# A decoder layer on one core: the order in which an instruction's waits are written

## What is computed

```
x = x + attn(layernorm(x))         # 16 heads, q and k are products of two linear maps, causal within a chunk
x = x + mixer(ctx, layernorm(x))   # conv, softplus step sizes, scan over 512 steps with 16 states, gate silu(z)
x = x + ffn(layernorm(x))          # bit_linear(silu(gate) * val), weights rounded to -1, 0, 1

def step(state, inp):              # the mixer's scan
    d, b, c, u = inp
    dA = jnp.exp(d[..., None] * A)
    state = state * dA + (d * u)[..., None] * b[:, None, :]
    y = jnp.einsum('bdn,bn->bd', state, c)
    return (state, y)
```

## Time and profile before

| | |
|---|---|
| median of 3 runs | 981.41 us (980.48 to 981.87) |
| span of the profiled execution | 979.3 us |
| TensorE busy | 811.0 us, 83% |
| VectorE busy | 790.5 us, 81% |
| ScalarE busy | 591.0 us, 60% |
| GpSimd busy | 478.2 us, 49% |
| chain that ended last | TensorE 47%, VectorE 28%, ScalarE 17% |

### The profile page before, as it was taken

One profiled execution on the slowest core, in us unless ns is written; L12 is line 12 of the kernel. 1 busy time (PEld: TensorE's weight loads), 2 busy tenths in 40 slices (PEclk: granted clock), 3 DMA queues, 4 the chain that ended last, 5 costly groups with the idle time before them and its releaser, 6 DMA issues.

```text
span 979.3 us, 11629 instructions
## 1 busy us (share of the span) xinstructions
PE 811.0 (83%) x4036; PEld 451.5 (46%) x4036; DVE 790.5 (81%) x932; ACT 591.0 (60%) x865; POOL 478.2 (49%) x283
## 2 busy tenths in 40 slices
PE   5778887548398888997988798998789899998798
PEld 2335555333263434565464344655455345664354
DVE  5879777577798988878798888787789998876874
ACT  3779779973457766355366766353356785533443
POOL 0447865685427534474347543356445645562020
PEclk8789797758699999988999899999799999999799
DMA  8676786867345543676535463565733555673000
GB/s 297 239 218 188 200 260 197 236 176 196 76 84 122 126 87 86 152 151 159 110 66 129 98 129 65 142 133 123 163 76 76 122 120 129 147 151 76 1 12 33
DMA packets 50495, 130.93 MB, mean 134 GB/s; under 512 B 7203, under 2 KB 7587, under 8 KB 50437
## 3 DMA queue, kind: packets, MB, share of 16 engines
q0 software_dynamic: 16128, 58.73, 31.6%
q1 hardware_dynamic: 34308, 71.45, 22.7%
HBM read 67.09 MB, written 4.35 MB: 73 GB/s over the span
## 4 chain that ended last, share of the span: by engine, by line
PE 47%; DVE 28%; ACT 17%; issue 6%; DMA 2%; DVEq 0%; SPq 0%; ACTq 0%
PE bank L839 18%; DVE W L1828 8%; PE bank L1054 6%; DVE PB L1817 5%; PE bank L868 4%; PE bank L887 4%; PE bank L1071 3%; ACT DEC L1294 3%; DVE U L1786 3%; DVE BST L1763 2%; PE bank L924 2%; PE bank L907 2%; PE bank L946 2%; DVE ARENA L1858 2%; DVE HAM L1974 1%
## 5 line engine op out<-in xcount | busy, mean ns | idle before, releaser
L1670 POOL TENSOR_TENSOR W<-W,CROW 128x1024 f32<-128x1024 f32 x128 | 317.6, 2481 | 226.4 <-DVE W L1828 195.9
L1828 DVE TENSOR_TENSOR_SCAN W<-DEC,PB 128x1024 f32<-128x1024 f32 x125 | 285.8, 2286 | 5.3 <-DVE PB L1817 1.0
L1817 DVE TENSOR_TENSOR PB<-DU,PB 128x1024 f32<-128x1024 f32 x128 | 156.5, 1223 | 21.6 <-PE PB L1009 17.5
L1683 POOL DMA_DIRECT2D ACC<-W x112 | 98.4, 878 | 146.7 <-DMA ACC<-W 124.9
L1294 ACT ACTIVATE DEC<-DT,ACOL 128x511 f32<-128x511 f32 x250 | 160.1, 710 | 15.1 <-DVE W L1828 14.1
L1054 PE MATMUL bank<-W,ARENA 128*128 128x512 fp8e4 x512 | 127.6, 394 | 0.0
L1249 ACT ACTIVATE ARENA<-bank 128x512 f32<-128x512 f32 x56 | 33.0, 593 | 90.3 <-PE bank L887 46.0
L1054 PEld LDWEIGHTS bank<-W,ARENA 128*128 128x128 bf16 x512 | 46.2, 100 | 64.4 <-issue 21.9
L1392 ACT ACTIVATE ARENA<-bank,SDQ 128x512 f32<-128x512 f32 x64 | 43.4, 686 | 47.5 <-PE bank L1054 47.2
L1966 DVE SCALAR_TENSOR_TENSOR ARENA<-bank,SDQ,ARENA 128x512 f32<-128x512 f32 x64 | 47.1, 741 | 27.1 <-ACT ARENA L1392 10.0
L868 PE MATMUL bank<-IDF,ARENA 128*128 128x128 f32 x384 | 55.2, 288 | 15.2 <-DVE ARENA L1845 5.9
(11 more groups left out here) (170 smaller groups left out, 1326.0 us busy)
## 6 DMA issues: line engine op xcount, KB each, us to landing
ACC<-W POOLq DMA_DIRECT2D x112, 512.0 KB, 4.6
CROW<-c_rows SPq DMA_DIRECT2D x98, 256.0 KB, 3.6
W<-in_wffn SPq DMA_DIRECT2D x27, 512.0 KB, 6.8
X<-in_wffn SPq DMA_DIRECT2D x21, 512.0 KB, 5.4
X<-in_x SPq DMA_DIRECT2D x7, 1024.0 KB, 8.8
out_dram<-X SPq DMA_DIRECT2D x16, 256.0 KB, 2.1
X<-in_ctxT SPq DMA_DIRECT2D x4, 512.0 KB, 5.1
ARENA<-in_x SPq DMA_DIRECT2D x1, 1024.0 KB, 5.8
```

Source lines behind the costliest of these rows:

```text
L1670: pool.tensor_tensor(w, w, CROW[k % 2][:, :].unsqueeze(1).broadcast_to([P, 2, L]), ALU.mult)\
L1683: pool.dma_start(ACC[accumulator(u)][:, :, :], w, accum_op=ALU.add).then_inc(y_summed, 16)
L1817: dve.tensor_tensor(into, du, rows, ALU.mult).then_inc(dbu_done.sem, 1)
L1828: dve.tensor_tensor_scan(flat(W[u % 4]), flat(decay_of(u)), flat(PB[:, scan_bank(u):scan_bank(u) + 2, :]), 0.0, ALU.mult, ALU.add).then_in ...
```

## The change

No instruction of an engine is added, removed or moved. Only waits are: the order in which they are written ahead of an instruction is turned around in some fifteen places, some are left out where an earlier one covers them, and on GpSimd some are written ahead of another instruction. The diff, cut to what the prediction speaks of (`reversed(...)` is put around the lists of drained banks in `up` and `largest` too, and `project_first`, `tile_T`, `scales_T`, `attend` and `gate_mixer` swap two waits in the same manner):

```
 def product(key, terms, ready=()):
-    for r in (R.free_at(*key), *ready):
+    for r in (*ready, R.free_at(*key)):
         pe.wait_ge(*r)
...
 def transposes(key, source, ready):
-    for r in (R.free_at(*key), *ready):
+    for r in (*ready, R.free_at(*key)):
...
 def kv(b, g):
-    for r in (R.free_at(*key), R.drained_at(b, "kfT", g), R.drained_at(b, "v", g)):
+    for r in (R.drained_at(b, "kfT", g), R.free_at(*key), R.drained_at(b, "v", g)):
...
 def abs_sums(i):
+    if i:
+        act.wait_ge(abs_done, i)
     act.wait_ge(w_abs[i % len(ABS_STAGE)], 16 * (i // len(ABS_STAGE) + 1))
-    act.wait_ge(abs_done, i)
...
 def outputs_c(u):
...
     b, h, n = unit(u)
+    if u < PAIRED and n % 2 == 0:
+        return
+    if transfers(u) > 1:
+        pool.wait_ge(y_summed, 16 * (transfers(u) - 1))
     pool.wait_ge(*hc_done.at(0, u + 1))
-    if opens(u):
+    if u == half_units(b, h)[1 if u < PAIRED else 0]:
         pool.wait_ge(*y_init.at(b, 2 * h + 2))
     if u < PAIRED:
-        if n % 2 == 0:
-            return
         pool.tensor_tensor(w, w, W[(u - 1) % 4][:, :, :], ALU.add).then_inc(pair_added, 1)
         pool.wait_ge(pair_added, u // 2 + 1)
-    if transfers(u) > 1:
-        pool.wait_ge(y_summed, 16 * (transfers(u) - 1))
     pool.dma_start(ACC[accumulator(u)][:, :, :], w, accum_op=ALU.add).then_inc(y_summed, 16)
...
 def inputs_b(u):
-    dve.wait_ge(*b_bcast.at(0, SPREAD_OF[u] + 1))
-    dve.wait_ge(*du_ready.at(b, 2 * h + 2))
+    if u:
+        dve.wait_ge(*scan_done.at(0, u))
+    if not joined(u):
+        dve.wait_ge(*b_bcast.at(0, SPREAD_OF[u] + 1))
+    if opens(u):
+        dve.wait_ge(*du_ready.at(b, 2 * h + 2))
...
-    if u:
-        dve.wait_ge(*scan_done.at(0, u))
...
 def feature(b, g, i):
+    dve.wait_ge(*R.drained_at(b, one, g))
     dve.wait_ge(*R.full_at(b, two, g))
-    dve.wait_ge(*R.drained_at(b, one, g))
...
 def gated(f, t, c):
+    if t and c == 2:
+        dve.wait_ge(*R.full_at(f, "hT", t - 1, 1))
+        dve.wait_ge(*R.full_at(f, "hT", t - 1, 0))
+    dve.wait_ge(*R.drained_at(f, "G", t, c))
     dve.wait_ge(*R.full_at(f, "V", t, c))
-    dve.wait_ge(*R.drained_at(f, "G", t, c))
-    if t and c == 2:
-        dve.wait_ge(*R.full_at(f, "hT", t - 1, 0))
-        dve.wait_ge(*R.full_at(f, "hT", t - 1, 1))
```

More of the change, by code:

```diff
@@ L915, in scores @@
                     R.begin(b, "S", g, h)
-                for r in R.all_drained_at((b, "k2", g)):
-                    pe.wait_ge(*r)
-                for h in heads:
+                if pair == 0:
+                    pe.wait_ge(*R.drained_at(b, "k2", g))
+                for h in reversed(heads):
                     pe.wait_ge(*R.free_at(b, "S", g, h))
@@ L934, in attend @@
                     R.begin(*key)
+                    pe.wait_ge(*R.drained_at(b, "kv", g))
                     pe.wait_ge(*R.free_at(*key))
-                    pe.wait_ge(*R.drained_at(b, "kv", g))
                     for c in range(1, TT):
@@ L964, in project_first @@
                 R.begin(*key)
-                for r in (R.free_at(*key), R.drained_at(b, "o", GROUPS - 2)):
+                for r in (R.drained_at(b, "o", GROUPS - 2), R.free_at(*key)):
                     pe.wait_ge(*r)
@@ L992, in tile_T @@
                 R.begin(*key)
-                for r in (R.free_at(*key), rp_step.at(f, 5 * (scale_group(t) + 1))):
+                for r in (rp_step.at(f, 5 * (scale_group(t) + 1)), R.free_at(*key)):
                     pe.wait_ge(*r)
@@ L1021, in scales_T @@
                 R.begin(*key)
+                pe.wait_ge(*rp_step.at(f))
                 pe.wait_ge(*R.free_at(*key))
-                pe.wait_ge(*rp_step.at(f))
                 for t in range(TT):
@@ L1039, in up @@
                 elif t == 0 and c == 0:
-                    for r in R.all_drained_at((f, "rT"), *((f, "xqT", k) for k in range(KT))):
+                    for r in reversed(R.all_drained_at((f, "rT"), *((f, "xqT", k) for k in range(KT)))):
                         pe.wait_ge(*r)
@@ L1970, in largest @@
             def largest(f, t, half):
-                for r in R.all_drained_at((f, "V", t, 2 * half), (f, "V", t, 2 * half + 1)):
+                for r in reversed(R.all_drained_at((f, "V", t, 2 * half), (f, "V", t, 2 * half + 1))):
                     dve.wait_ge(*r)
@@ L2034, in gate_mixer @@
             def gate_mixer(f):
+                dve.wait_ge(y_summed, 16 * transfers((f + 1) * UNITS - 1))
                 dve.wait_ge(*sz_ready.at(f))
-                dve.wait_ge(y_summed, 16 * transfers((f + 1) * UNITS - 1))
                 for h in range(2):
```

## The result

The changed kernel takes **978.39 us** (median of 11 runs, 976.27 to 981.17) against 980.48 (979.56 to 982.19) of the kernel before, run beside it. The ratio is 0.9973 with an interval of 0.9964 to 0.9982: 2.6 us less, with 1.8 to 3.5 by that interval. The forecast was 979.3, 2.1 us less than the 981.41 it started from.

A forecast was written before the change was run, and what follows sets the result against it. No engine alone bounds it; nearly full TensorE and VectorE hand work over. Terms 1.3 + 0.8 + 0.2 - 0.2 = 2.1 us off 979.3 gave span 977.2, plus 2.1 to the run median: 979.3 us, own range 978.6 to 981.0.

The forecast's parts named there:

- The price on VectorE: Scan to next multiplication: a last-met wait in a two-wait sequencer instruction costs 0.10 us more than one carried.
- The VectorE sum, 1.3 us: VectorE's reordered waits on the chain: 0.9 + 0.83 saved, 0.14 and 0.28 lost, net 1.3 us less.
- The TensorE sum, 0.8 us: First matmuls behind input or bank waits: 19 chain places gain, 6 lose, net 13 x 0.06 = 0.8 us less.
- Row 0, 0.2 us lost: GpSimd in row 0: pair addition waits for the last transfer, so 0 to 1.8 us extra, taken as 0.2.
- the scan at 113.31: VectorE scan on the chain in row 0, forecast to lose 0 to 1.8 us waiting for a late transfer.
- The third rival: Row 0's pair additions come 9.4 us late and VectorE pays: sign decided from 2.1 us on, up to 988.5; chance 0.13.
- ScalarE, 0.2 us: The wait of abs_sums for the sum before it: 4 places on the chain, 0.2 us less.
- GpSimd from row 1 on, nothing: GpSimd's transfers carry y_summed after row 0: some issues sooner, some later, no cost or gain on the chain.
- The second rival, every place counts: Places off the chain on VectorE, TensorE and ScalarE count too: 5.7 us in all, time 975.7; chance 0.12.
- The sum, 2.1 us: Whole kernel: 1.3 + 0.8 + 0.2 - 0.2 = 2.1 us less, a change of 0.21%.

The follow-up runs named there:

- the small dose: Changed kernel with the scan's wait for its multiplication back in a sequencer instruction at 126 places: 981.04 us, against 978.90 for the changed kernel on the third chip.
- VectorE's part alone: Kernel before with only VectorE's edits (multiplication, feature, gated, largest, gate of the mixer): 979.94 us against 981.40, ratio 0.9984.
- TensorE's part alone: Kernel before with only TensorE's edits, the bank's wait written after the input's: 981.27 us, ratio to before 0.9997.
- the TensorE dose: Changed kernel with three or four extra long-met sequencer waits behind those of each product and transpose group, from row 1 on: 988.85 us, ratio to before 1.0068.
- the kernel by place: Changed kernel with row 0's addition ahead of the wait and the last-met wait written first at 52 places: 977.22 us, ratio to before 0.9961.
- GpSimd's part alone: Kernel before with only GpSimd's edits: transfer carries the previous transfer's wait, row 0's pair addition behind it: 981.13 us, ratio 1.0003.
- row 0 turned back: Changed kernel with row 0's pair addition ahead of the transfer's wait again: 976.55 us, ratio to before 0.9942; changed kernel beside it 976.26.

## Why the prediction was right, and where it was not

**The price on VectorE.** Right: 0.12 became 0.02 behind a scan. The Trainium skill, in VectorE: DVE Perf Modes, The DRAIN you can't avoid, says that between VectorE instructions the semaphore costs nothing extra. For the carried wait the traces agree (0.02). For one in the sequencer they do not: the small dose had 0.054 more at each scan, and the kernel was 2.4 us (0.5 to 4.3) slower. The measurement decides.

**The VectorE sum, 1.3 us.** Right in sign and, within a wide interval, in size: VectorE's part alone gave 1.6 (0.4 to 2.7). But its trace has 2.7 us of gain between 174 and 222 us and 1.1 in the stage where the six matmuls kept the upper clock. That the places alone make up the 1.3 is not shown.

**The TensorE sum, 0.8 us.** The gaps shortened as forecast (22 of 0.14 in the chain became 6), but what they are worth is not settled. TensorE's part alone gave 0.3, the interval from 1.8 less to 1.2 more. The dose shows that some places do cost something there. But the kernel by place, which should have won back 9 such places and 7 of VectorE's, won nothing.

**Row 0, 0.2 us lost.** The first half was right: pair additions idle for 2.22 and 1.94 us, a scan waits 1.02, and an idle time for ScalarE takes it up. The path of the loss was wrong. The forecast put it at the scan at 113.31, which waits for nothing; it came by SyncE's queue, a weight load issued 1.24 us later that ScalarE and then VectorE waited for, 0.5 us with GpSimd's part alone, won back later. The size at the end can't be told from zero: 0.3 more (0.7 less to 1.3 more) with GpSimd's part alone, and nothing gained with row 0 turned back. That the small term fits is therefore luck as much as insight. The third rival, with 2.1 us and more, has fallen. That the changed trace gives back 0.79 us between 36 and 174 us is one execution, in which ScalarE waited 1.70 for that load; two others of the same kernel gain 0.42 and 0.44 there.

**ScalarE, 0.2 us, and GpSimd from row 1 on, nothing.** Neither was tried alone.

**Two slips of the working.** The 2.1 us from span to time set a median against one execution; each listed run is about 1.8 above its own span. And half way from 979.3 to the second rival's 975.7 is 977.5, not 976.8. Neither moves the result out of the forecast.

**The second rival, every place counts.** It would have been 5.7 us less. The small dose, VectorE's part and the TensorE dose speak against it as a mechanism. Yet one chip of three gave 6.0 less by the ratio, 976.26 us, below the forecast's range.

**The sum, 2.1 us.** The number came out: 2.6 less (1.8 to 3.5) on the first chip and 2.6 on the third. How it came about did not. The sum read the gain as a shift that is added up place by place and is the same in each execution; the traces show a small shift and steps from TensorE's clock, a term that the forecast did not have. That the two agree in size is in part luck. Look at 545 to 550 us, by the windows view, in before, after, and the changed kernel on the third chip:

```profile
545.00:550.00 5.00, 5.00 (x17) 2.70 (x16) 3.66 (x3) 1.99 (x3) 1.91 (x2) 0.50 0.45 84
```

```profile
545.00:550.00 5.00, 5.00 (x19) 2.73 (x18) 3.18 (x3) 2.06 (x3) 3.13 (x2) 0.56 0.40 77
```

```profile
545.00:550.00 5.00, 5.00 (x27) 2.63 (x26) 3.88 (x3) 2.64 (x4) 3.24 (x2) 0.89 0.55 104
```

and the VectorE instruction that waits for it, in the timelines of the latter two:

```profile
549.04 0.75 DVE L1969 SCALAR_TENSOR_TENSOR ARENA<-bank,SDQ,ARENA 128x512 f32<-128x512 f32 x1 [1.82 <-PE bank L868]
```

```profile
547.59 0.75 DVE L1969 SCALAR_TENSOR_TENSOR ARENA<-bank,SDQ,ARENA 128x512 f32<-128x512 f32 x1 [0.58 <-PE bank L868]
```

Same program, same stage. With the granted clock at 0.89 instead of 0.56 TensorE gets through 27 matmuls and not 19, and VectorE's wait is 0.58 and not 1.82. That step of 1.2 us is more than half of the whole forecast. The execution on the second chip has it too (clock 1.00 in this window), and a larger one between 174 and 222 us. That these steps coincide with the clock is shown. Why the changed kernel takes them in some executions, and why more of them on one chip, is not: I only argue that an earlier start of a stretch can bring the clock's rise forward by a step. The times of the third chip fit. Of before's 23 runs there the nine with a mean granted clock of 0.904 or more took 979.32 to 980.24 us, and the fourteen below it 980.91 to 982.90. The changed kernel's twelve spread wider, from 974.65 to 981.52, and the mean clock doesn't sort them as well: 975.37 has 0.907 and 981.20 has 0.906. On the two other chips with before's clocks listed the two groups of before overlap a little. So the clock goes with part of the spread, and the rest has no known cause.

## What to carry to other kernels

Write first the wait that is met last at the places on the chain, and count those rather than all places: the price per place is 0.05 to 0.10 us on VectorE, and the small dose fits the chain's count (2.4 us, with 0.5 to 4.3, against 2.0) and not that of all places (6.8). When a wait is moved, follow it into the other queues too: the cost here came by a load that stood behind another one in SyncE's queue. An effect of this size is better confirmed by doses than by undoing it, since 1.1 of the 2.6 us here stand where TensorE's clock did not fall, and even a dose of 2 us can hold such a step. Before trusting a sum of small hand-overs, cut two traces at the same instructions and see whether the saving grows evenly or in steps.

## What the runs showed of the hardware that I had not expected

- The cost of a sequencer instruction of two waits is not fixed: 0.10 us more than the carried wait between scan and multiplication, 0.054 between multiplication and scan. Each further one whose waits were long met added about 0.1 on VectorE (a gap of 0.48 us with four of them), and on TensorE three or four together 0.45.
- Six matmuls of 128x512 took 2.84 us at a granted clock of 1.00, and 4.17 to 4.30 us in the four traces with a lowered clock at that place. An idle time for TensorE of 1.82 us becomes 0.58 from one execution of the same program to another, at granted clocks of 0.56 and 0.89 in the 5 us window.
- Of added idle time ahead of the scans, about a third reached the end at 0.054 a place (2.4 of 6.8 us, with 0.5 to 4.3), and 62% at about 0.45 (33.7 of 54.4).
